# The root of the query norm moved out of the queries: into the scale of the exponentials and of the row maximum

## The reference, cut to what matters

```
q = l2norm(q) * qs                  # per row and head (64 wide)
k = l2norm(k) * ksc
q, k = rotary_xpos(q, k)            # position tables, linear in q and in k
sim = einsum('bhwid,bhwjd->bhwij', bq, bk)
sim = where(mask, -big, sim)
attn = softmax(sim, axis=-1)
out = einsum('bhwij,bhwjd->bhwid', attn, bv)
```

## Time and profile before

| what | value |
|---|---|
| median of 3 runs | 1334.16 us (1333.44 to 1335.03) |
| the profiled execution | 1331.52 us, span of the profile 1329.7 us |
| granted clock of TensorE, mean | 0.998 of full speed |
| busy share of PE, ACT, POOL, DVE | 95%, 87%, 85%, 83% |
| first layer's attention | about 20 to 530 us |
| feed-forward of the first layer, gates of the recurrent layer | about 530 to 680 us |
| second layer's attention | about 680 to 1205 us |
| feed-forward of the second layer and the output | about 1205 to 1330 us |

### The profile page before, as it was taken

How to read it: one execution, slowest core, us unless ns; L and a number is a source line. 1 busy time by engine, 2 the same in 40 slices (tenths; PEclk the granted TensorE clock), 3 DMA queues, 4 the chain that set the end, 5 groups by cost and what they waited for, 6 DMA issues and landing times.

```text
span 1329.7 us, 38195 instructions
## 1 busy us (share of the span) xinstructions
PE 1261.0 (95%) x13793; PEld 1009.5 (76%) x13794; DVE 1107.6 (83%) x1924; ACT 1160.4 (87%) x3529; POOL 1133.9 (85%) x831
## 2 busy tenths in 40 slices
PE   7889999999999998999988999999999999999997
PEld 4777888888888887666756788888888888876775
DVE  6788888888888886688878999998899999984777
ACT  5878999999999998776768899999999999998886
POOL 4888999999999987376689999999999999984775
PEclk9999999999999999999999999999999999999999
DMA  5222222222322211010011111111222111110222
GB/s 165 53 54 61 69 61 61 61 73 65 80 70 54 53 38 34 16 44 25 1 29 38 45 45 45 46 45 46 51 51 50 46 46 45 37 38 25 77 76 86
DMA packets 60299, 70.05 MB, mean 53 GB/s; under 512 B 8912, under 2 KB 38288, under 8 KB 60112
## 3 DMA queue, kind: packets, MB, share of 16 engines
q1 hardware_dynamic: 60112, 67.61, 20.2%
HBM read 13.33 MB, written 4.19 MB: 13 GB/s over the span
## 4 chain that ended last, share of the span: by engine, by line
PE 73%; ACT 7%; issue 5%; POOL 5%; DVE 5%; DMA 2%; SPq 1%; ACTq 0%; DVEq 0%; POOLq 0%
PE ps L182 58%; PE ps L243 8%; PE ps L253 3%; PE ps L256 3%; ACT P L631 3%; POOL t L1219 2%; DMA norm<-X 1%; POOL hxr L1219 1%; DVE t L947 1%; POOL P L1219 1%; DVE t L956 1%; DVE nm L975 1%; ACT sqk L605 1%; DVE sums L963 1%; ACT Vn L645 1%
## 5 line engine op out<-in xcount | busy, mean ns | idle before, releaser
L631 ACT ACTIVATE P<-ps,nm 128x128 f32<-128x128 f32 x1024 | 363.5, 384 | 3.9 <-DVE nm L975 3.9
L182 PE MATMUL ps<-wqkv,hT 128*128 128x512 f32 x1152 | 326.9, 426 | 13.1 <-DVE t L947 10.0
L1219 POOL TENSOR_TENSOR P<-P,rden 128x512 f32<-128x512 f32 x256 | 296.2, 1164 | 43.7 <-DVE rden L982 42.9
L1219 POOL TENSOR_TENSOR t<-t 128x1024 f32<-128x1024 f32 x128 | 307.1, 2399 | 30.2 <-DVE t L947 28.9
L182 PEld LDWEIGHTS ps<-wqkv,hT 128*128 128x128 f32 x1152 | 214.8, 188 | 89.6 <-issue 28.1
L1219 POOL TENSOR_TENSOR t<-t,rr 128x1024 f32<-128x1024 f32 x128 | 243.4, 1901 | 16.5 <-ACT rr L614 16.4
L631 ACT ACTIVATION_READ_ACCUMULATOR P<-ps,nm 128x1 f32 x1024 | 230.9, 226 | 0.0
L1219 POOL TENSOR_TENSOR hxr<-hxf,hxr 128x512 fp32r<-128x512 f32 (+1 forms) x94 | 128.6, 1396 | 87.3 <-ACT hxr L687 87.3
L956 DVE TENSOR_TENSOR t<-ps,tabl 128x512 f32<-128x512 f32 x256 | 164.2, 683 | 38.5 <-ACT sqk L605 38.1
L621 ACT ACTIVATE PT<-ps 128x1024 f32<-128x1024 f32 x128 | 130.4, 1019 | 63.3 <-PE ps L243 62.2
L975 DVE TENSOR_REDUCE nm<-ps 128x4 f32<-128x512 f32 x256 | 173.7, 680 | 5.1 <-PE ps L182 5.1
(11 more groups left out here) (131 smaller groups left out, 2553.6 us busy)
## 6 DMA issues: line engine op xcount, KB each, us to landing
Vs<-Vn SPq DMA_DIRECT2D x224, 128.0 KB, 2.3
side<-in_x SPq DMA_DIRECT2D x16, 256.0 KB, 3.0
A<-X SPq DMA_DIRECT2D x16, 256.0 KB, 2.5
norm<-X SPq DMA_DIRECT2D x32, 128.0 KB, 2.3
oT<-in_x SPq DMA_DIRECT2D x16, 256.0 KB, 2.9
out<-oT SPq DMA_DIRECT2D x16, 256.0 KB, 2.2
norm<-X SPq DMA_DIRECT2D x32, 127.8 KB, 2.4
hsh<-X SPq DMA_DIRECT2D x31, 128.0 KB, 2.2
```

The lines of the kernel that those rows point to most:

```text
L182: return e.matmul(o, lhsT, rhs, start=start, stop=stop, skip_group_check=True)
L631: k = act(P[:, g, :], ps[:, 3 + s, (g % 4) * 128:(g % 4 + 1) * 128], ACT.Exp, bias=nm[:, g:g + 1], accum_out=den[:, g:g + 1])
L1219: return e.tensor_tensor(o, a, b_, op)
```

## The change

The query root is no longer multiplied into the queries. `scale_qk` on POOL covers the 8 key heads only (512 elements in each partition). PE transposes the queries as soon as they are added (`s_add`) and waits for `s_tn` only ahead of the keys. The similarities of a row are then too large by the inverse of a positive number of that row, so DVE multiplies the negated maximum by the root before it is the bias (a new instruction in `row_max`, with a new tile `mx8` and a new semaphore `s_mx`), and the exponentials take the root as their scale. `rr` gets a second buffer, since the roots of a tile are now read until its exponentials.

```diff
-        rr = sb("rr", [128, 16])
+        rr = sb("rr", [128, 2, 16])
+        mx8 = sb("mx8", [128, 8])
...
+        def q_root(n):
+
+            return rr[:, n % 2, 0:8].rearrange("p (c s) -> p s c", s=2)
...
             def turn_qk(l, i):
                 n = l * NT + i
                 c0 = tq[i % 2]
-                e.wait_ge(s_tn, n + 1)
+                e.wait_ge(s_add, n + 1)
                 if n > 1:
                     e.wait_ge(s_PT, n - 1)
                 for c in range(4):
                     k = e.transpose(ps[:, 5, c * 128:(c + 1) * 128], c0[:, c * 128:(c + 1) * 128], idf[:])
                 k.then_inc(s_tpq, 1)
+                e.wait_ge(s_tn, n + 1)
                 for c in range(4):
                     k = e.transpose(ps[:, 6, c * 128:(c + 1) * 128], c0[:, (4 + c) * 128:(5 + c) * 128], idf[:])
...
             def norm_rt(l, i):
                 n = l * NT + i
                 e.wait_ge(s_ss, n + 1)
-                if n:
-                    e.wait_ge(s_tn, n)
-                act(rr[:], ss[:], ACT.Ln, scale=65536.0).then_inc(s_rr0, 1)
+                if n > 1:
+                    e.wait_ge(s_tn, n - 1)
+                    e.wait_ge(s_e, 2 * n - 2)
+                act(rr[:, n % 2, :], ss[:], ACT.Ln, scale=65536.0).then_inc(s_rr0, 1)
...
             def exps(l, i, s):
...
+                e.wait_ge(s_rr, n + 1)
                 e.wait_ge(s_nm, 2 * n + s + 1)
                 for g in range(4 * s, 4 * s + 4):
                     k = act(P[:, g, :], ps[:, 3 + s, (g % 4) * 128:(g % 4 + 1) * 128], ACT.Exp,
-                            bias=nm[:, g:g + 1], accum_out=den[:, g:g + 1])
+                            scale=q_root(n)[:, s, g % 4:g % 4 + 1], bias=nm[:, g:g + 1], accum_out=den[:, g:g + 1])
...
             def row_max(l, i, s):
...
-                e.tensor_reduce(nm[:, 4 * s:4 * s + 4], S4, AX, ALU.max, negate=True).then_inc(s_nm, 1)
+                e.tensor_reduce(mx8[:, 4 * s:4 * s + 4], S4, AX, ALU.max, negate=True).then_inc(s_mx, 1)
+                e.wait_ge(s_rr, n + 1)
+                e.wait_ge(s_mx, 2 * n + s + 1)
+                e.tensor_tensor(nm[:, 4 * s:4 * s + 4], mx8[:, 4 * s:4 * s + 4], q_root(n)[:, s, :], ALU.mult).then_inc(s_nm, 1)
...
             def scale_qk(l, i):
                 n = l * NT + i
-                v = heads(tq[i % 2])
+                v = heads(tq[i % 2])[:, HEADS:, :]
                 e.wait_ge(s_add, n + 1)
                 e.wait_ge(s_rr, n + 1)
-                tt(v, v, rr[:].unsqueeze(2).to_broadcast([128, 16, DH]), ALU.mult).then_inc(s_tn, 1)
+                tt(v, v, rr[:, n % 2, HEADS:].unsqueeze(2).to_broadcast([128, HEADS, DH]), ALU.mult).then_inc(s_tn, 1)
```

More of the change, by code:

```diff
@@ L167, in program @@
             sem(n_) for n_ in ("s_dec", "s_rt0", "s_rt", "s_osq", "s_rms0", "s_rms", "s_s", "s_th"))
-        s_cst, s_tabm, s_t2, s_ss0, s_ss, s_nm, s_rd, s_kt, s_wlo, s_w2lo, s_h0, s_hxlo1 = (
-            sem(n_) for n_ in ("s_cst", "s_tabm", "s_t2", "s_ss0", "s_ss", "s_nm", "s_rd", "s_kt", "s_wlo", "s_w2lo", "s_h0", "s_hxlo1"))
+        s_cst, s_tabm, s_t2, s_ss0, s_ss, s_mx, s_nm, s_rd, s_kt, s_wlo, s_w2lo, s_h0, s_hxlo1 = (
+            sem(n_) for n_ in ("s_cst", "s_tabm", "s_t2", "s_ss0", "s_ss", "s_mx", "s_nm", "s_rd", "s_kt", "s_wlo", "s_w2lo", "s_h0", "s_hxlo1"))
         s_bn, s_st, s_dcy, s_dk, s_xadd, s_hc, s_hn, s_b1g, s_gh, s_oa = (
@@ L609, in norm_rt @@
                 e.wait_ge(s_ss, n + 1)
-                if n:
-                    e.wait_ge(s_tn, n)
-                act(rr[:], ss[:], ACT.Ln, scale=65536.0).then_inc(s_rr0, 1)
+                if n > 1:
+                    e.wait_ge(s_tn, n - 1)
+                    e.wait_ge(s_e, 2 * n - 2)
+                act(rr[:, n % 2, :], ss[:], ACT.Ln, scale=65536.0).then_inc(s_rr0, 1)
                 e.wait_ge(s_rr0, n + 1)
-                act(rr[:], rr[:], ACT.Exp, scale=-0.5, bias=ln2x8).then_inc(s_rr, 1)
+                act(rr[:, n % 2, :], rr[:, n % 2, :], ACT.Exp, scale=-0.5, bias=ln2x8).then_inc(s_rr, 1)
             def keep_p(l, i):
```

## The result

The change makes the kernel slower: 1550.70 us median of 4 runs (1547.58 to 1551.52) against 1334.60 us (1333.44 to 1335.58), a ratio of 1.1615 with a 95% interval of 1.1595 to 1.1635. The profiled execution took 1551.52 us, with a span of 1549.7 us.

The account below looks back on a forecast made before the run. PE was taken as the bound, with DVE to replace it: +1.66 us a tile in layer 0 and +1.64 in layer 1, over 62 tiles each, add 205 us to 1331.5; with 2.6 for the median, 1539 us, range 1465 to 1605.

Parts of the forecast that it names:

- The second product: DVE's product behind the second maximum, ready in the midst of POOL's sum, ends only after it: +1.90 us a tile.
- The first product: DVE's product behind the first maximum: +0.21 us a tile, plus 0.4 us held by POOL (bounds 0 and 1.03).
- No cost of the scale operand: ACT's exponentials with one more operand: taken as 0, at most 0.02 us each, 0.16 us a tile.
- the ring through ACT: Layer 0 loop from exponentials through rotation, first maximum and second product back to exponentials: 8.73 us without the 0.4.
- my sum: DVE's own time a tile in layer 0: 6.63 plus 0.21, 0.4 and 1.90 is 9.14 us; 8.2 without extra work.
- POOL's saving: POOL's product with the roots halved, 0.87 us a tile less: worth at most PE's stall in layer 1, 13 us.
- The copy inside `kT` is held less: DVE's copy in layer 1, behind POOL's shorter product: 0.1 us a tile less.
- The small product does not slip in: Rival denied here: the 4-element product is not held by POOL and PE stays the bound; 1326 us, chance 0.08.
- POOL's sum is not late: Rival denied here: POOL's sum starts late, holding DVE up to some 0.4 us a tile longer; 1589 us, chance 0.06.
- The granted clock: Rival: PE's waits in every tile lower its clock; 2270 us, or about 1800 with half the time lower; chance 0.02.

Follow-up runs that it names:

- e4_product_only: Kernel before the change, plus a DVE product of the maxima by ones behind each maximum and nothing else: 1602.25 us, ratio 1.1998.
- e3_scale_only: Kernel before the change, with a column of ones as scale operand of the exponentials and nothing else: 1384.22 us, ratio 1.0368.
- e8_product_keys: e4_product_only with POOL's product with the roots on the 8 key heads only, the queries' norm left out: 1529.00 us, ratio 1.1467.
- e7_key_tail_layer1: Kernel before the change; in layer 1 alone, the copy inside kT replaced by a copy of the last 64 keys from PSUM one tile earlier: 1328.96 us.
- e2_split_sum: Changed kernel, with POOL's sum issued as two instructions of 512 elements instead of one of 1,024: 1429.73 us, ratio 1.0719.
- e6_key_tail: Kernel before the change; in both layers, the copy inside kT replaced by a copy of the last 64 keys from PSUM one tile earlier: 1335.61 us.
- e1_columns: Changed kernel, with each product of 4 elements replaced by four one-column tensor_scalar instructions with the root as pointer: 1430.54 us, ratio 1.0717.
- e9_keys_only: Kernel before the change, with POOL's product with the roots on the 8 key heads only, the queries' norm left out: 1320.43 us, ratio 0.9909.

## Why the prediction was right, point by point

It said 1539 us in 1465 to 1605, and the median is 1550.7.

- *The second product is held by POOL's sum.* Right, and shown from three sides: another form of the same product (-120 us), another size of POOL's instruction (-121 us), the product alone (+268 us). I had the hold at 1.87 us (1.84 to 3.71); the median duration is 1.79, since the product starts 0.08 us later than I had it and ends with the sum all the same.
- *The first product.* I took a hold of 0.4 us. The mean duration of 0.40 less the unheld 0.16 leaves 0.24. But both products start 0.10 us behind their maximum (305.76 to 305.87 in the tile shown), not 0.03. In `e4_product_only`, whose product waits for the maximum alone and not for the roots as well, it is 0.03 us. From the start of the first maximum to the rotation's last part the mean over 44 tiles of each layer is 1.09 and 1.15 us instead of 0.60: +0.49 and +0.55, where I had +0.61. That two of my errors go against each other here is luck.
- *No cost of the scale operand.* The step that failed. I bounded it at 0.02 us an exponential; it is 0.093 us. The Trainium skill has the figure (ScalarE: Activation LUTs, section "What ACT_TABLE_LOAD costs"): each pointer operand adds about 93 ns to an activation. The trace of `e3_scale_only` agrees (0.435 - 0.342 us).
- *What the operand did to the pace.* In the ring through ACT it counts four times. In the tile shown the ring is: product's end to exponentials 0.12 us (300.45 to 300.57), to the rotation 3.31 (303.88), to the first maximum 1.20, to the rotation's last part 0.87, to the second product's end 3.72 (309.67). That is 9.22 us, where I had 0.08 + 2.93 + 1.20 + 0.81 + 3.71 = 8.73; 0.38 of the 0.49 us are the exponentials' part. Of 44 turns of layer 0 (tiles 10 to 53), the rotation waits for ACT in 22, and their mean pace is 9.23 us; that of the other 22, in which DVE has extra work, is 10.04, where my sum implied 2 x 9.14 - 8.2 = 10.08. So layer 0 was 9.63 us and not 9.44, and this is the 12 us by which the forecast was low: 62 x 0.19. In layer 1 the rotation never waits for ACT in 44 turns, and the ring doesn't show: 9.7 forecast, 9.69 measured, and 9.71 in `e8_product_keys`, which has no scale operand. In layer 0 `e8_product_keys` has 9.42 us, and in its turns in which DVE waits for ACT 2.94 us from the exponentials to the rotation. By itself the operand costs 50 us. Its price within the change was not isolated: `e8_product_keys` is 22 us faster than the changed kernel, but it also lacks the root's second buffer, the earlier transposes and the second wait, and over half of layer 0's difference lies in the turns in which DVE doesn't wait for ACT (9.76 us there, 10.04 here).
- *POOL's saving is worth at most 13 us.* Right by itself (-13), though `e7_key_tail_layer1` shows that only about half of it is the copy that I named; the other half needs POOL to be earlier with its normalisation. With the product in place it is worth 73 us (1602 to 1529): the first products, held by POOL's product, last 0.89 us in the mean with the whole one and 0.39 us with the half.
- *The copy inside `kT` is held less.* I took 0.1 us a tile off in layer 1 for it. It lasts 1.04 us there instead of 1.15, once in four tiles, which is 0.03 us a tile. In layer 0 it lasts 1.02 us instead of 0.52, 0.12 us a tile more on DVE, where I had nothing. The layer's sum came out in spite of it.
- *Rivals.* The small product does not slip in, save for a few at the starts and ends of the layers. POOL's sum is not late: it starts 0.08 us behind the rotation in the median, and over 0.12 us behind it in 7 of 128 tiles. The granted clock is 1.00 in both windows of attention; its mean over the span fell from 0.998 to 0.984, and the loss lies in the first 200 us (0.97), from 560 to 860 us (0.94 to 0.97) and from 1400 us on (0.97). PE's waits in these windows, 1.33 us in the tile shown, did not bring it down. In `e4_product_only`, whose tiles are longer still, the mean is 0.972 and that of 200 to 500 us 0.96, inside the first layer's attention; what that costs was not tried.

One reading was off by a name and changes nothing: in the earlier trace rows only the maximum runs beside POOL's sum, and the rotation beside its product with the roots.

What stays open is the order in which DVE and POOL come to their turn. In the kernel before, the layer norm's product got in between POOL's two normalisations, and in `e2_split_sum` most second products got in between the two halves of the sum; in `e6_key_tail` the layer norm's product waited for both, and in `e4_product_only` 11 products waited for two instructions. No run here tells which of these happens when. Open as well is what makes up the 46 us that `e1_columns` and `e2_split_sum` are slower than the kernel before beyond the 50 of the scale operand.

## What to carry to other kernels

Before a tiny DVE instruction goes between a release and the work that it releases on POOL, look at where its operands lie: with two tiles in SBUF it cost here not its 0.16 us but the rest of what POOL was doing. Read this from durations, not from waits, since no semaphore shows it: compare the maximum of a line's durations with its minimum. And an operand from memory in the hottest instruction of an engine near its bound is a cost to look up, not to take as nothing.

## What was not expected of the hardware

- A DVE instruction with two SBUF inputs can be held over two POOL instructions in a row: 3.20 us for 4 elements in `e4_product_only`, 2.55 us for 512 in `e6_key_tail`.
- Two SBUF inputs are not the only case. The copy inside `kT` has one, and lasts 1.14 us in layer 1 of the kernel before, behind POOL's normalisation, and 0.41 us in `e9_keys_only`. The head sums, which also go from SBUF to SBUF, last 1.20 to 1.21 us in all 128 cases of the changed kernel, and the columns of `e1_columns` at most 0.22 us.
- An exponential of 128 columns with scale and bias from memory starts 0.093 us later behind its like than one with a bias alone (0.435 against 0.342 us).
- A product that waits for two semaphores began 0.10 us after its maximum, one that waits for one of them 0.03 us after (`e4_product_only`). Whether the second wait is the reason was not tried by itself.
